# Decoder layer on one core: two swaps in a step's order and a reordered beginning

## The reference

```python
# 1: attention, 16 heads of 8 columns; keys and values through a latent of 32 columns
latent_kv = (x @ W_k + x @ W_v) @ W_down_kv
k_rec, v_rec = latent_kv @ W_up_k, latent_kv @ W_up_v
scores = einsum('bhqd,bhkd->bhqk', x @ W_q, k_rec) / sqrt(128) * decay
x = layernorm(x + softmax(scores) @ v_rec @ W_o)
# 2: attention over channels: per head an 8 by 8 matrix x^T ctx, softmax, applied to ctx @ Wv.T + bv
x = layernorm(x + that @ Wo.T + bo)
# 3: layer norm, router of 8 experts, the best 2 of each row, each expert a gated
#    network 128 -> 512 -> 128 with a layer norm of its own; sum by the gates
x = layernorm(x + ffn(x))
```

## Time and profile before

| | |
|---|---|
| three runs | 592.62, 592.98 and 595.98 us; median 592.98 us |
| the profiled execution | 591.37 us; its span, first to last instruction, 589.6 us |
| busy, share of the span | PE 527.6 us (89%), DVE 496.1 us (84%), ACT 419.5 us (71%), POOL 370.9 us (63%) |
| mean granted TensorE clock | 0.981 of full speed |
| chain that ended last | PE 58%, DVE 16%, issue 14%, ACT 6%, DMA 3% |

### The profile page before, as it was taken

How to read it: one execution, slowest core, us unless ns; L and a number is a source line. 1 busy time by engine, 2 the same in 40 slices (tenths; PEclk the granted TensorE clock), 3 DMA queues, 4 the chain that set the end, 5 groups by cost and what they waited for, 6 DMA issues and landing times.

```text
span 589.6 us, 17958 instructions
## 1 busy us (share of the span) xinstructions
PE 527.6 (89%) x5148; PEld 438.5 (74%) x5148; DVE 496.1 (84%) x1548; ACT 419.5 (71%) x1179; POOL 370.9 (63%) x708
## 2 busy tenths in 40 slices
PE   3799999999999999999978888978999999999395
PEld 2577787777877778777657777867898888888295
DVE  2689999999999999999996878889888888877353
ACT  2599998898988989889777654463566666765134
POOL 4325678888888888888877646653544344333344
PEclk9899999999999999999999999998999999999789
DMA  6313213232331311311005445653666666664283
GB/s 178 56 47 81 44 40 92 53 94 50 88 87 58 92 53 48 87 58 56 30 17 173 150 121 161 187 177 107 192 202 187 182 202 203 207 192 153 90 281 94
DMA packets 78933, 68.83 MB, mean 117 GB/s; under 512 B 17092, under 2 KB 60804, under 8 KB 78836
## 3 DMA queue, kind: packets, MB, share of 16 engines
q1 hardware_dynamic: 73748, 57.77, 34.7%
q0 software_dynamic: 4320, 9.15, 4.6%
q10 hardware_dynamic: 768, 0.75, 0.4%
HBM read 52.85 MB, written 14.80 MB: 115 GB/s over the span
## 4 chain that ended last, share of the span: by engine, by line
PE 58%; DVE 16%; issue 14%; ACT 6%; DMA 3%; ACTq 1%; another core or an unknown queue 0%; SPq 0%; DVEq 0%; POOL 0%; POOLq 0%
PE ps_m L845 7%; PE ps_t L785 5%; PE ps_s L785 5%; PE ps_s L825 4%; PE ps_s L827 4%; PE ps_t L827 3%; PE ps_t L825 3%; DVE hid L1461 3%; DVE rinv L1201 3%; PE ps_m L730 2%; ACT sil L1090 2%; PE ps_m L700 2%; PE ps_m L720 2%; PE ps_m L682 2%; PE ps_m L761 2%
## 5 line engine op out<-in xcount | busy, mean ns | idle before, releaser
L845 PEld LDWEIGHTS ps_m<-wot,hid 128*128 128x128 f32 x568 | 83.9, 192 | 20.4 <-issue 7.7
L578 POOL DMA_INDIRECT expert_out<-yt,dest x71 | 70.7, 996 | 43.8 <-issue 23.8
L845 PE MATMUL ps_m<-wot,hid 128*128 128x128 f32 x568 | 91.2, 280 | 7.0 <-DVE yt L1472 3.4
L1025 ACT ACTIVATE sc<-sc,rowmax 128x128 f32<-128x128 f32 x256 | 77.9, 389 | 1.0 <-DVE rowmax L1195 1.0
L1195 DVE TENSOR_REDUCE rowmax<-sc 128x8 f32<-128x1024 f32 x64 | 76.8, 1203 | 0.3 <-issue 0.3
L549 POOL DMA_INDIRECT expert_in<-xhat,pos x64 | 65.0, 1015 | 16.1 <-issue 15.4
L1083 ACT ACTIVATE x2c<-ps_s,prt 128x256 f32<-128x256 f32 (+1 forms) x78 | 35.4, 454 | 54.3 <-PE ps_s L827 48.3
L502 POOL TENSOR_TENSOR sc<-sc,rowmax 128x1024 f32<-128x1024 f32 x32 | 60.7, 1895 | 10.0 <-DVE rowmax L1195 8.7
L1083 ACT ACTIVATE x2c<-ps_t,prt 128x256 f32<-128x256 f32 (+1 forms) x78 | 35.3, 452 | 34.1 <-PE ps_t L827 28.1
L825 PE MATMUL ps_s<-xg,w2t 128*128 128x256 f32 (+1 forms) x156 | 46.5, 380 | 8.5 <-DVE hid L1461 6.7
L568 POOL COPY bot<-bo_rows 128x128 f32 x39 | 11.7, 301 | 60.8 <-DVE yt L1472 60.7
(11 more groups left out here) (283 smaller groups left out, 1576.7 us busy)
## 6 DMA issues: line engine op xcount, KB each, us to landing
w2t<-in_L_ffn_W_dram SPq DMA_DIRECT2D x39, 256.0 KB
w1t<-in_L_ffn_W_dram SPq DMA_DIRECT2D x39, 256.0 KB
wot<-in_L_ffn_Wo_dram SPq DMA_DIRECT2D x39, 256.0 KB
kbd<-key_image SPq DMA_DIRECT2D x29, 256.0 KB
xst<-expert_in SPq DMA_DIRECT2D x32, 137.0 KB
g<-expert_out SPq DMA_DIRECT2D x7, 512.0 KB, 9.1
call<-in_ctx_dram SPq DMA_DIRECT2D x8, 256.0 KB
out_dram<-xall SPq DMA_DIRECT2D x16, 128.0 KB, 1.8
```

Of the source, the lines that this page charges most:

```text
L578: pool.indirect_dma_start(ys_dram[:, :], bass.IndirectOffsetOnAxis(ap=dest[:, n, a:a + 1], axis=0), yt[:, par, a, :], None).then_inc(y_out ...
L845: mm = pe.matmul(ps_y(i)[:, a * P:(a + 1) * P], hid[:, par, c, a * P:(a + 1) * P], wot[:, par, c, :], start=(c == 0 and a == 0), stop=(c = ...
L1025: done = act.activation(sc[:, slot, h, :], sc[:, slot, h, :], ACT.Exp, bias=rowmax[:, slot, h:h + 1])
```

## The change

Four edits, in the order of the diff (its line numbers differ from those of before).

1. SP takes over the six transfers that ACT issued last: the four of W_o stand behind the load of x[1:4], with a semaphore of their own (`ld_wo`) that PE waits for at the first projection; the two that zero the key image stand behind the fills.
2. In a POOL step `choices` comes ahead of `biased_sum`.
3. On PE the first transpose of x comes between the second and the third product of the weights, on ACT its copy between the two copies; the first two products use another PSUM bank (ps_s).
4. In a DVE step `decayed_scores(s + 2, 0)` comes ahead of `shift4(s - 4)`.

```diff
@@ sync
                 sp.dma_start(xall[:, 1:4, :], x[1:4].rearrange("b s d -> s b d")).then_inc(ld_x[0], 16)
+                for j in range(GH):
+                    sp.dma_start(wo[32 * j:32 * j + 32, :],
+                                  W_o.rearrange("(r j d) n -> j r d n", r=GRP, j=GH)[j]).then_inc(ld_wo, 16)
...
                     if b == AT_ONCE:
                         rows_of_none()
+                        sp.wait_ge(zeroed, 1)
+                        for i in range(2):
+                            sp.dma_start(kimg[i].rearrange("(p n) -> p n", p=P), zrow[:, :]).then_inc(k_clear, 16)
                         sp.wait_ge(k_clear, 32)
@@ gpsimd
                     if ever(s - 7): scatter(s - 7)
+                    if ever(s - 5) and s < B: choices(s - 5)
                     if ever(s - 2): biased_sum(s - 2)
-                    if ever(s - 5) and s < B: choices(s - 5)
                     if ever(s - 3): router_rows(s - 3)
@@ tensor
-                    pe.wait_ge(ld_w, 16 * 7)
+                    pe.wait_ge(ld_w, 16 * 3)
...
+                    if b == 0:
+                        pe.wait_ge(ld_wo, 16 * GH)
                     pe.matmul(m0a, attT[:, :], wo[:, :], start=True, stop=False)
...
+                pe.wait_ge(cst, 2)
+                pe.wait_ge(su_v, 1)
+                pe.transpose(ps_s[:, 0, 0, :], setup[:, 0, :], ident[:, :]).then_inc(su_p, 1)
+                pe.wait_ge(su_a, 1)
+                pe.wait_ge(ld_k, 16 * 2)
+                pe.matmul(ps_s[0:DL, 0, 0, :], setup[:, 4, 0:DL], setup[:, 1, :], start=True, stop=True).then_inc(su_p, 1)
+                trans_x(first_step)
+                pe.wait_ge(su_a, 2)
+                pe.matmul(m1a, setup[0:DL, 0, :], setup[0:DL, 5, :], start=True, stop=True).then_inc(su_p, 1)
+                pe.wait_ge(su_a, 3)
...
-                    if ever(s + 2): trans_x(s)
+                    if ever(s + 2) and s > first_step: trans_x(s)
@@ scalar
                 act.dma_start(setup[:, 3, :], xWo).then_inc(ld_w, 16)
-                for j in range(GH):
-                    act.dma_start(wo[32 * j:32 * j + 32, :],
-                                  W_o.rearrange("(r j d) n -> j r d n", r=GRP, j=GH)[j]).then_inc(ld_w, 16)
-                for i in range(2):
-                    act.dma_start(kimg[i].rearrange("(p n) -> p n", p=P), zrow[:, :]).then_inc(k_clear, 16)
...
+                copy(setup[0:DL, 0, :], ps_s[0:DL, 0, 0, :]).then_inc(su_a, 1)
+                copy_x(0)
+                act.wait_ge(su_p, 3)
+                copy(wkf[:, :], m1a).then_inc(su_a, 1)
...
@@ vector
                     if ever(s - 2): norm2(s - 2)
+                    if ever(s + 2): decayed_scores(s + 2, 0)
                     if ever(s - 4): shift4(s - 4)
-                    if ever(s + 2): decayed_scores(s + 2, 0)
                     if ever(s): heads(s)
```

More of the change, by code:

```diff
@@ L167, in decoder_layer @@
         ld_x = [sem("ld_x_even"), sem("ld_x_odd")]; ld_c = [sem("ld_c_even"), sem("ld_c_odd")]
-        ld_w = sem("ld_w"); ld_k = sem("ld_k"); ld_x0 = sem("ld_x0"); ld_p = sem("ld_p"); ld_e = sem("ld_e")
+        ld_w = sem("ld_w"); ld_wo = sem("ld_wo"); ld_k = sem("ld_k"); ld_x0 = sem("ld_x0"); ld_p = sem("ld_p"); ld_e = sem("ld_e")
         cst = sem("cst"); rcst = sem("rcst"); su_v = sem("su_v"); su_p = sem("su_p"); su_a = sem("su_a")
@@ L1131, in expert_step @@
                         beside(i, 4)
+                act.wait_ge(su_p, 1)
+                copy(setup[:, 1, :], ps_s[:, 0, 0, :]).then_inc(su_a, 1)
+                act.wait_ge(su_p, 2)
+                copy(setup[0:DL, 0, :], ps_s[0:DL, 0, 0, :]).then_inc(su_a, 1)
+                copy_x(0)
+                act.wait_ge(su_p, 3)
+                copy(wkf[:, :], m1a).then_inc(su_a, 1)
                 for s in range(first_step, B + 2):
-                    if ever(s + 1): copy_x(s + 1)
+                    if ever(s + 1) and s > -1: copy_x(s + 1)
                     if ever(s - 2): exp_half(s - 2)
```

## The result

The changed kernel takes 578.6 us (median of four runs, 576.8 to 580.2), the kernel before 594.2 beside it (four runs, 592.6 to 596.0): a ratio of 0.976, with a 95% interval of 0.972 to 0.979. The profiled execution took 580.02 with a span of 578.3, against 591.37 and 589.6: 11.3 less in the span. By the medians the gain is 15.6, since the profiled execution of before lies 2.8 under the median of its four runs and that of the changed kernel 1.4 over its own. The three other runs of the changed kernel had spans of 574.9 to 578.4. The forecast was 581.2 by the median and 579.6 for the profiled execution, in a range of 577 to 587.

What follows compares the result with a forecast made beforehand. It took the loop to be bound by a ring of DVE and POOL (9.16 us a step) and the beginning by ACT's transfer issues. 3.9 + 6.7 + 1.2 = 11.8 us less gave 581.2 by the median, 579.6 profiled, range 577 to 587.

Steps and rivals of the forecast that it cites:

- The hold: DVE's `shift4`, two SBUF inputs, stands until POOL's long addition ends; one place back it is held 0.1 instead of 0.57.
- The beginning: Start of the kernel: ACT, freed of six issues, copies 3.1 earlier, and x between the products gives 0.75; 3.9 us.
- the rung: Start, PE and ACT: taking x between the weights' products removes one serial stage before the keys, net 0.75 us.
- no obstacle: Start: x[0] lands at 4.8 and its transpose comes up at about 5.0, so its load delays nothing.
- The store of batch 3's keys: On SP, behind the wait for the zero transfers: 1.5 us late, at worst 6.7; price nothing, at worst 0.4.
- The second swap: `choices` ahead of the biased sum on POOL: `oh` no longer held, DVE saves another 0.21 us a step.
- The added wait: POOL's biased sum queues behind a wait for DVE, ending about 224.9 against PE's need at 226.12: 1.2 us of cover.
- The loop: The 24 steps fall from a mean of 9.23 to 8.95 us, 0.28 less each, 6.7 us in all.
- POOL's own pace: POOL alone, without its 0.29 of waiting, needs 8.87 us a step and is the next bound; 8.95 with some waiting.
- PE's ladder stays: Rival: PE's part of a step doesn't shorten, only 0.15 at the handover goes; 8.5 us gained, 584.5; chance 0.25.
- The other steps: Four steps outside the 24 (s = 4 and the last three), where DVE is late: 0.3 each, 1.2 us.
- The sum: Whole kernel: 3.9 + 6.7 + 1.2 = 11.8 us less, with nothing later taking it back.

Runs made afterwards that it cites:

- e5_one_input: The kernel before with `shift4` in its old place, written with one tensor input and a per-partition scalar: 588.74 us, ratio 0.990.
- e1_begin: The kernel before with only the new beginning (transfers, first x, the products' new place), neither swap: 587.44 us, ratio 0.991.
- e11_no_x: The changed kernel with the first x back behind the weights' products on PE and ACT, the six transfers still on SP: 585.37 us, ratio 0.983.
- e2_shift: The kernel before with only the DVE swap, `shift4` behind the decayed scores: 584.03 us, ratio 0.983.
- e4_swaps: The kernel before with both swaps (`shift4` and `choices`) and the old beginning: 582.99 us, ratio 0.981.
- control: The changed kernel, unedited, run again beside the last kernels: 583.11 us, ratio 0.980 to the kernel before.
- third group: The last kernels run together on one chip, the unedited changed kernel and variants of it, with their own runs of the kernel before: median 595.2 us.
- e12_both_shorter: The changed kernel with the biased sum over 64 of 128 columns from the second batch on and seven of eight exponentials: 583.24 us, ratio 0.979.
- e10_gram_later: The changed kernel with the masked gram on DVE behind the second multiplication of the decayed scores: 587.11 us, ratio 0.985.

## Why the prediction was right, step by step

**The hold.** Right, with its cause (e5_one_input). "Held by 0.1 instead of 0.57" came out as 0.05 in the step shown. Beside the last addition, where it came up only 1.1 us behind the addition's start, `shift4` was still caught, for 0.79.

**The beginning.** Forecast 3.9, with 3.1 for ACT's copy and 0.75 for the rung. Measured: 3.06 for the copy, 3.68 at the first keys, 3.5 at the first of the 24 additions, 4.0 in the span of e1_begin. The 3.1 isn't all passed on, since PE then waits for W_up_k and, with the weight load of x's transpose (0.38), for x: it lands at 4.99 and its transpose starts at 5.27, so "no obstacle" was not quite so. e11_no_x has 2.9 for the transfers, and the rung is worth 0.6 to 1.0. The sum is right.

**The store of batch 3's keys.** Forecast near 23, it starts at 22.07, 0.19 behind its copy of keys (21.62 + 0.26 = 21.88), where before it was 0.08 behind. The second transfer of zeros was issued at 16.61 and landed at 22.06, so the wait cost about 0.1 there. The scores of batch 3 at 33.48 are 3.55 earlier than before, as much as everything around them. Hidden, as forecast.

**The second swap.** Here a step of the reasoning failed, though the sum didn't. The prediction gave `oh` another 0.21 of DVE's time by its new place. e2_shift shows that the first swap alone takes that hold away, because `oh` comes up 0.5 earlier, before the biased sum. The 0.5 stands in the prediction, but its effect on the old order was not followed. The added wait is small: 1.6 us of POOL in all between 60 and 280 us (9.4 against 7.8), and the biased sum ends in the step shown at 216.14, 5.42 behind the addition's start, instead of 4.89. It lies in cover: e4_swaps, which has it, is not slower a step than e2_shift, which has not.

**The loop.** Forecast 8.95 a step by POOL's own pace, measured 8.942: 24 x 0.288 = 6.9 against 6.7. In the step shown POOL waits for DVE only in front of `both`, for 0.09, and not before its addition, and DVE only 0.19. But that step comes round in 8.80, less than the 8.87 that the prediction took for POOL's own pace: that figure was too high, and the mean came out right because other steps are longer. That POOL bounds the step of 8.94 was not tested, as both kernels with a shorter POOL ran where PE's signal is late. There the step stays at 9.04, POOL waits longer before its additions (2.9 us instead of 1.5), and a shorter POOL gives nothing. That is near the rival "PE's ladder stays", with 0.25: it let a step gain 0.15, and there a step gains about 0.19 (9.230 to 9.043). What holds it is the late signal of PE, which the prediction did not have.

**The other steps.** Forecast 1.2, measured 11.5 at the last addition (305.18 to 293.69) less 3.5 and 6.9: 1.0.

**The sum.** 11.8 against 11.3 in the pair of profiles. The medians of the first comparison differ by 15.6, and by 12.1 in the control's group (595.2 to 583.1). So the agreement with the pair of profiles within 0.5 is luck in part: against the forecast median of 581.2 the measured one lies 2.6 lower. Of the 3.5 between the groups the slower step can account for 2.4 (24 x 0.1). The rest lies within what the end of the program moves from one execution to another, some 3 us. Two profiles of the third group show that, control and e12_both_shorter. Up to 286 us their additions lie within 0.35 of each other, at the last addition they are 1.4 apart, and the spans are 585.1 and 582.0. Granted clock and busy times by stretch (us, PE, PEld, DVE, ACT and POOL busy, granted clock, DMA share, GB/s), control first:

```profile
280.00:340.00 60.00, 50.08 (x451) 42.58 (x450) 46.26 (x169) 42.14 (x101) 39.83 (x85) 0.93 0.37 109
340.00:400.00 60.00, 51.93 (x296) 45.59 (x295) 48.26 (x165) 27.89 (x57) 32.74 (x57) 0.93 0.46 139
```

```profile
280.00:340.00 60.00, 47.66 (x455) 39.88 (x454) 46.52 (x173) 41.81 (x101) 40.45 (x85) 0.98 0.36 110
340.00:400.00 60.00, 52.85 (x310) 46.43 (x309) 48.71 (x168) 28.47 (x58) 32.58 (x59) 0.96 0.50 152
```

The control was granted 0.93 of the clock in both stretches, the other 0.98 and 0.96, and the control has fewer matmuls done by 400 us. That the lower clock falls in one execution and not in the other is seen, its cause is not. For e10_gram_later, too, a loss of 4 us against the control stands beside equal steps; its own part in that is open.

**Left open.** Why PE's signals come 1.0 late in one set of profiles and not in the other. No run changed PE's own work. The starts of PE's matmuls, counted from the addition, agree within 0.07 us up to that point, and their ends are modelled, so whether the matmuls or only the signals are late can't be read. Also, every fifth step or so is 0.2 to 0.4 longer in all kernels.

## What to carry to other kernels

Look for tiny instructions with long medians: a product of one element per partition that takes 0.72 instead of 0.15 is standing, and if it ends where a long operation of POOL ends, its second SBUF input is the first suspect. Move it by one place, or give it one tensor input and a scalar per partition. Then follow what is later in the same queue before costing a second edit: here the first move cured the second hold too. And when a shortening seems to make a kernel slower, run the unedited kernel beside it, in the same group of runs, before explaining it. And a clock of 1.00 in a view says little ahead of the trace's first clock record: compare the length of one matmul with that of the same matmul later.

## What the runs showed of the hardware

- A DVE instruction of 128x1 with two SBUF inputs stood 0.57 us for a POOL addition of 128x1024 and ended with it; with one tensor input and a per-partition scalar it took 0.201 to 0.212 in all 32 places. A one-hot of 128x16 that started beside an indirect transfer and ended 0.07 to 0.54 us ahead of it took 0.174 to 0.177.
- Not every POOL operation with two SBUF inputs holds such an instruction: beside a root of 128x1 (0.55 us) the 128x1 product took 0.139, starting 0.16 behind it.
- One program had a pace of 8.94 us in its first profile and of 9.04 in the control's, at equal granted clock (1.00 from 60 to 280 us in both). In the slower one four signals of PE came up to 1.1 us behind the ends of their matmuls in 21 steps, and DVE waited for the first of them.
- At the beginning matmuls took about twice as long as later (eight transposes 1.92 against 1.04) until the trace's first clock record. The moment, and with it 1.0 us, differed between two kernels whose matmuls started alike until then (29.45 and 27.01 us).
